# One-hots of a graph convolution compared as bf16 pairs, and three moved pieces of work beside a feed-forward

## The reference, cut to what matters

```python
h = segment_sum(h1[src] * norm, dst)          # first convolution, 8 features
h = relu(layernorm(h) ...)
out = relu(segment_sum((h @ W2)[src] * norm, dst) + b2)   # second convolution
x = x + out * size_factors
x = x + down(silu(gate(layernorm(x))) * up(layernorm(x)))  # 512 -> 1408 -> 512
```

## Time and profile before

| what | value |
|---|---|
| time, median of 3 runs | 3543.81 us (3538.64 to 3545.29) |
| time of the profiled execution | 3537.91 us |
| its span, first to last instruction | 3536.2 us |
| PE / DVE / ACT / POOL busy, share of the span | 79% / 56% / 30% / 58% |
| part with second convolution and feed-forward | about 802 to 2190 us |
| its one-hot comparisons (L171) | 49 times, 842.8 to 2040.3 us |

### The profile page before, as it was taken

How to read it: one execution, slowest core, us unless ns; L and a number is a source line. 1 busy time by engine, 2 the same in 40 slices (tenths; PEclk the granted TensorE clock), 3 DMA queues, 4 the chain that set the end, 5 groups by cost and what they waited for, 6 DMA issues and landing times. The chain is left out here.

```text
span 3536.2 us, 58101 instructions
## 1 busy us (share of the span) xinstructions
PE 2806.9 (79%) x16521; PEld 2050.4 (58%) x16522; DVE 1977.7 (56%) x3616; ACT 1074.2 (30%) x1721; POOL 2059.1 (58%) x2157
## 2 busy tenths in 40 slices
PE   6855655213999999999999996778887878788799
PEld 6855544212788877787878886333333434335687
DVE  8888898966354545454454543433344344443676
ACT  3445555003233323323233323001121212223454
POOL 0077777767777777777700001777777777772454
PEclk9678778556999999999999998899999999998899
DMA  3222232002233333333322324777777877775564
GB/s 104 59 63 53 49 100 46 5 4 53 46 105 96 100 90 105 91 85 101 85 90 92 102 83 135 219 225 232 224 235 238 244 231 244 233 242 174 174 212 129
DMA packets 237217, 459.14 MB, mean 130 GB/s; under 512 B 80060, under 2 KB 102828, under 8 KB 236994
## 3 DMA queue, kind: packets, MB, share of 16 engines
q0 software_dynamic: 111360, 235.84, 25.8%
q1 hardware_dynamic: 125634, 220.46, 19.2%
HBM read 389.41 MB, written 73.25 MB: 131 GB/s over the span
## 5 line engine op out<-in xcount | busy, mean ns | idle before, releaser
L1814 POOL DMA_INDIRECT rows<-xn_rows,srcT x784 | 742.3, 947 | 273.1 <-issue 244.8
L122 POOL DMA_INDIRECT msg_c<-hid_rows,srcT x752 | 727.4, 967 | 244.1 <-issue 230.1
L1965 PE MATMUL pV<-rows,oh 128*128 x2240 | 554.9, 395 | 144.7 <-issue 49.6
L122 POOL DMA_INDIRECT msg_b<-hid_rows,srcT x464 | 455.0, 981 | 149.3 <-issue 137.7
L1965 PEld LDWEIGHTS pV<-rows,oh 128*128 x2240 | 223.8, 100 | 461.6 <-issue 290.2
L1388 PE MATMUL acc<-wd,hT 128*128 128x512 f32 x1617 | 399.6, 395 | 0.0
L1363 PE MATMUL pG<-xT,wgu_hi 128*128 128x512 f32 (+1 forms) x1232 | 373.1, 385 | 10.1 <-issue 8.4
L1363 PE MATMUL pU<-xT,wgu_hi 128*128 128x512 f32 (+1 forms) x1232 | 362.9, 376 | 0.0
L1388 PEld LDWEIGHTS acc<-wd,hT 128*128 128x128 f32 x1617 | 301.3, 188 | 67.9 <-issue 8.8
L2278 DVE SCALAR_TENSOR_TENSOR oh<-ids,bases,dstT 128x896 f32 x160 | 184.2, 1151 | 211.0 <-issue 145.4
L2266 DVE TENSOR_TENSOR agg<-agg,pV x161 | 110.2, 685 | 335.7 <-PE pV L1965 335.3
(11 more groups left out here) (393 smaller groups left out, 4549.7 us busy)
## 6 DMA issues: line engine op xcount, KB each, us to landing
wd<-wd_rows SPq DMA_DIRECT2D x154, 512.0 KB, 3.6
we<-in_L_ffn_expert_w SPq DMA_DIRECT2D x16, 1024.0 KB, 8.4
x_rows<-xr SPq DMA_DIRECT2D x49, 256.0 KB, 4.6
xn_rows<-pair SPq DMA_DIRECT2D x49, 256.0 KB, 2.0
rows<-xn_rows,srcT POOLq DMA_INDIRECT x784, 3.8
res<-x_rows SPq DMA_DIRECT2D x49, 256.0 KB
x_rows<-agg SPq DMA_DIRECT2D x49, 256.0 KB, 4.3
xt<-in_x SPq DMA_DIRECT2D x48, 256.0 KB, 2.7
```

Source lines behind the costliest of these rows:

```text
L122: nc.gpsimd.indirect_dma_start(msg[:, c, :], None, table, bass.IndirectOffsetOnAxis(ap=srcT[:, c:c + 1], axis=0)).then_inc(landed[u % 2], 16)
L1814: nc.gpsimd.indirect_dma_start(rows[:, u % RING, c, :], None, xn2_rows, bass.IndirectOffsetOnAxis(ap=srcT[:, u * Q + c:u * Q + c + 1], axi ...
L1965: last = nc.tensor.matmul(pV[:, ds(to, 1), :].rearrange("p a d -> p (a d)"), oh[:, ds(to, 1), c, :].rearrange("p a d -> p (a d)"), rows[:, ...
```

## The change

Four things. (1) In the second convolution only, a unit first subtracts the tile's first row number (`first_id`, one fp32 per partition) from 20 numbers of `dstT` and writes them as bf16 (`rel`); the comparison then has two bf16 operands in SBUF, `numbers` (0 to 127, each twice) and `rel`, and is laid out so that two chunks lie side by side: the innermost dimension is the pair. After each tile 128 is added to `first_id` instead of to `tiota`. (2) The matmuls take a chunk's matrix from the pairs, at every second element. (3) `tile_range` of a unit moves out of `build` into `prepare`, which in the steps lies between DVE's product and its difference; these are now two functions, `up` and `low`. (4) `scale_rows` moves from (1, 1) to (2, 0), which is behind the build at (1, 2), and `rows` from (2,0), (3,0), (4,0), (5,0) to (3,0), (3,1), (4,0), (4,1).

```diff
@@ build_unit, with c0 and units as arguments
         nc.vector.tensor_tensor(lo, rest[:], mid, ALU.subtract)
-        nc.vector.tensor_tensor(onehot[:], bc(tiota.unsqueeze(1), (P, U, P)),
-                                bc(dstT[:, at].unsqueeze(2), (P, U, P)), ALU.is_equal).then_inc(ready, 1)
+        nc.vector.tensor_scalar(rel, dstT[:, at], first, None, ALU.subtract).then_inc(related, 1)
+        dve.wait_ge(related, n + 1)
+        full = (P, U // 2, P, 2)
+        nc.vector.tensor_tensor(onehot, bc(numbers.unsqueeze(1), full), bc(rel.rearrange("p (g j) -> p g j", j=2).unsqueeze(2), full),
+                                ALU.is_equal).then_inc(ready, 1)
@@ sum_columns
-            last = nc.tensor.matmul(acc[j * HX:j * HX + H3, :], mstage[:, k, :], onehot[:, k, :], start=False, stop=False)
+            last = nc.tensor.matmul(acc[j * HX:j * HX + H3, :], mstage[:, k, :], onehot[:, k // 2, :, k % 2], start=False, stop=False)
@@ groups
-    first = {(FB - 1, 2): [(part.build, 0)]}
+    first = {(FB - 1, 0.5): [(part.prepare, 0)], (FB - 1, 2): [(part.build, 0)]}
+        (j, 0.5): [(part.prepare, j)] for j in (1, 2, 3)} | {
-    behind = {(2 + j, 0): [(part.rows, j)] for j in range(4)} | {
+    behind = {(3 + j // 2, j % 2): [(part.rows, j)] for j in range(4)} | {
         (0, 0): [(part.residual, None)],
         (0, 2): [(part.stats_rows, None)],
-        (1, 1): [(part.scale_rows, None)]}
+        (2, 0): [(part.scale_rows, None)]}
             part.up(i, g, f)
+            beside(f, 0.5)
+            part.low(i, g, f)
             beside(f, 1)
@@ tensors and VectorE of the part
-            tiota = pb(ctx, "tiles_c", [P, 512], F32)[:, 0:P]
+            first_id = sb(ctx, "first_id", [P, 1], F32)
+            numbers = sb(ctx, "numbers_c", [P, P, 2], BF16)[:]
+            rel = sb(ctx, "rel_c", [P, U], BF16)[:]
+            pairs = onehot[:].rearrange("p u n -> p (u n)").rearrange("p (g n j) -> p g n j", n=P, j=2)
-                own.step(nc.vector.tensor_copy(tiota, iota[:]))
+                own.step(nc.vector.tensor_copy(numbers, bc(iota[:].unsqueeze(2), (P, P, 2))))
+                own.step(nc.vector.memset(first_id[:], 0.0))
+                def prepare(i, k, j):
+                    at_tile.append(tile_range(dve, ranges, i * G + k))
-                    own.step(nc.vector.tensor_scalar_add(tiota, tiota, float(P)))
+                    own.step(nc.vector.tensor_scalar_add(first_id[:], first_id[:], float(P)))
```

More of the change, by code:

```diff
@@ L152, in chunk_at, with build_unit @@
     return ds(at, size)
-def build_unit(nc, dve, t, units_done, ranges, dstT, tiota, onehot, msg, rest, mstage, split, ready, used, msg_ready):
-    c0, units = tile_range(dve, ranges, t)
+def build_unit(nc, dve, c0, units, units_done, dstT, first, numbers, rel, onehot, msg, rest, mstage, split, related, ready, used, msg_ready):
     with dve.Fori(0, units) as b:
@@ L310, with __init__ @@
 class Part:
-    def __init__(self, gate=nothing, up=nothing, down=nothing, build=nothing, sums=nothing, layer1=nothing,
+    def __init__(self, gate=nothing, up=nothing, low=nothing, down=nothing, prepare=nothing, build=nothing, sums=nothing, layer1=nothing,
                  stats=nothing, scale=nothing, norm=nothing, turn=nothing, residual=nothing, stats_rows=nothing, scale_rows=nothing,
@@ L316, in __init__ @@
                  enter=nothing, leave=nothing):
-        self.gate, self.up, self.down = gate, up, down
+        self.gate, self.up, self.low, self.down = gate, up, low, down
+        self.prepare = prepare
         self.build, self.sums, self.layer1 = build, sums, layer1
@@ L1171, in program @@
             "tail lanes ohs prod masked reduced parts far small_in nv_clear msg fence fence_sp fence_pe fence_dve onehot used split agg own_rows aggT conv relu "
-            "x1 var std rs xn xT_ps xT_hi xT_lo gate_ps up_ps silu hmul h_hi h_lo down x2 var2 std2 rs2 "
+            "related x1 var std rs xn xT_ps xT_hi xT_lo gate_ps up_ps silu hmul h_hi h_lo down x2 var2 std2 rs2 "
             "xn2 row_hi row_lo dve".split())}
@@ L1336, in sums @@
                         wait_alone(pe, s["aggT"], T, s["fence_pe"])
-                    sum_columns(nc, pe, T, units_done, ranges, own_rows[:, j, :], mstage, identb, zerob, acc, onehot,
+                    sum_columns(nc, pe, T, units_done, ranges, own_rows[:, j, :], mstage, identb, zerob, acc, pairs,
                                 s["onehot"], s["used"]).then_inc(s["agg"], 1)
@@ L1516, in _ @@
                 units_done = tally(dve, "units_done2")
+                at_tile = []
+                def prepare(i, k, j):
+                    at_tile.append(tile_range(dve, ranges, i * G + k))
                 def build(i, k, j):
@@ L1521, in build @@
                     nc.vector.tensor_copy(own_rows[:, j, :], own3[:, ds(T, 1), :].rearrange("p a b -> p (a b)")).then_inc(s["own_rows"], 1)
-                    build_unit(nc, dve, T, units_done, ranges, dstT, tiota, onehot, msg, mrest, mstage, s["split"], s["onehot"], s["used"], s["msg"])
-                    own.step(nc.vector.tensor_scalar_add(tiota, tiota, float(P)))
+                    build_unit(nc, dve, *at_tile.pop(), units_done, dstT, first_id[:], numbers, rel, pairs, msg, mrest, mstage, s["split"], s["related"], s["onehot"], s["used"], s["msg"])
+                    own.step(nc.vector.tensor_scalar_add(first_id[:], first_id[:], float(P)))
                 def layer1(i, k, j):
@@ L1573, in up, with low @@
                     nc.vector.tensor_tensor(sil[:, 0:n], pU[:, 0:n], sil[:, 0:n], ALU.mult).then_inc(s["hmul"], 1)
+                def low(i, g, f):
+                    step, n, slot = steps_before(i, g, f), len(GROUPS[g]) * P, (g * FB + f) % 2
                     dve.wait_ge(s["hmul"], step + 2)
@@ L1597, in rows @@
                     nc.vector.tensor_tensor(pair[:, k % 2, 1, :], xn[:, j % 2, :], pair[:, k % 2, 0, :], ALU.subtract).then_inc(s["row_lo"], 1)
-                groups(dve.Fori, Part(build=build, layer1=layer1, stats=stats, scale=scale, turn=turn, up=up,
+                groups(dve.Fori, Part(prepare=prepare, low=low, build=build, layer1=layer1, stats=stats, scale=scale, turn=turn, up=up,
                                       residual=residual, stats_rows=stats_rows, scale_rows=scale_rows, rows=rows,
```

## The result

The changed kernel takes 3506.22 us (median of 6 runs, 3500.2 to 3516.2), the kernel before 3539.37 us beside it (6 runs, 3530.4 to 3545.3). By the medians that is 33 us less. The ratio is 0.9911, 95% interval 0.9894 to 0.9929, which is 25 to 38 us of 3539: faster, and clear of the scatter. The profiled execution takes 3501.57 us, against 3537.91.

What follows compares the result with a forecast made beforehand. PE sets the time (busy 1108 of 1152 us), waiting for DVE's late one-hots. From 3537.9 us, 4.6 (first four tiles) and 32.7 (six groups) leave 3500.6; plus 5.9 for the median, 3506.5, said as 3507; range 3490 to 3524.

Steps and rivals of the forecast that it cites:

- Register work, 0.65: DVE's builds: moving tile_range's load and register operations into prepare takes 0.65 us off the gap before the first cast.
- A build, 5.60 to 3.85: DVE's build of a one-hot: 5.60 us less 0.65 register work, less 1.32 comparison, plus 0.22 rel, makes 3.85.
- The start of the chain, left at 1186.9: Step 2 of a three-tile group: build 1 starts at 1186.9, ready at 1190.75, before PE comes at 1192.16.
- The waits of 1.25 in step 4 and 1.3 before `layer1` 0: Three-tile groups: PE waits 1.25 us for one-hot 3, then 1.3 before layer1 0 for ACT's late copy.
- rival (b): Three-tile groups: no new waits in steps 4 and 5, 15 us less, 3492 in all; chance 0.15.
- First four tiles, 4.6: Serial tiles before the first group: shorter builds gain 4.8 us, less 0.2 for new constants, so 4.6.
- No port blocking: DVE's comparison beside POOL's gathers: two SBUF inputs cause no blocking, counted as nothing; by the skill's rule, near 3519.
- Rival (c): DVE's comparison stands behind a gather, up to 0.94 us each, 12 us in all, 3519; chance 0.08.
- (d): PE's one-hot matmuls: four strided streams read at half rate, 14 us, some of it hidden, 3519; chance 0.10.
- (g): PE's one-hot matmuls: four column groups lose their overlap, 20 take 1.17 us instead of 0.29, 3550; chance 0.02.
- Rival (e): SP's queue in three-tile groups: wd comes late by 1.5 us in six groups, 3516; chance 0.07.
- (f): DVE's comparison: the fast form isn't taken, a build is 5.2 us, perhaps 6 us remain, 3538; chance 0.03.

Runs made afterwards that it cites:

- experiment 4: Changed kernel with the register work (tile_range) back in build: steps 2 to 6 of six three-tile groups 235.0 us, ratio 0.9937 to the kernel before.
- experiment 3: Changed kernel with the old comparison (fp32 row numbers in PSUM, no pairs): steps 2 to 6 of six three-tile groups 239.9 us, ratio 0.9931 to the kernel before.
- experiments 5 to 7: Changed kernel with scale_rows back, 225.7 us; changed kernel with rows back, 226.0; kernel before with row numbers in SBUF, 257.3 and 257.1 (steps 2 to 6, six groups).

## Why the prediction was right, point by point

The time (3507 against 3506.2), the sign and the reason (DVE's one-hots came late, and a shorter build takes the waits away) were right. Its picture of steps 4 and 5 was not.

- **Comparison, 1.49 us; `rel`, 0.22.** 1.49 in the median and 0.23. The pair rate of L533 and L535 carried over exactly.
- **Register work, 0.65.** Mis-sized: put back, it costs 0.7 to 0.9 a build, as experiment 4 shows. The load and the operations of the earlier trace rows sum to 0.52, and the gaps beside them were put too low.
- **A build, 5.60 to 3.85.** In the group shown it is 3.6 (1185.61 to 1189.20) for build 1, 3.3 for build 2 (behind the difference that ends at 1193.56) and 3.1 for build 3 (behind the remainder that ends at 1201.56). The three are 0.3 to 0.7 short of 3.85 each, 1.6 together.
- **The start of the chain, left at 1186.9.** The prediction let build 1 start where the difference of step 1 had ended, 1.26 us behind the beginning of step 2. It has no term for build 0, which lies in the last step of the group before and gets shorter too. DVE comes to `residual` 2.2 us earlier against the gate of step 1 (1177.34 with the gate at 1179.33; 1174.86 with the gate at 1179.03), and the difference of step 1 ends at 1185.61, only 0.30 behind step 2. That is 0.96 us more for the chain, and the second to fifth of the six groups agree: 1.26 to 1.36 before, 0.27 to 0.30 after. From DVE's timelines, before and after:

```profile
1177.34 2.48 DVE L1582 TENSOR_TENSOR xr<-xr,acc 128x512 f32<-128x512 f32 x4
...
1174.86 2.48 DVE L1600 TENSOR_TENSOR xr<-xr,acc 128x512 f32<-128x512 f32 x4
```

- **The waits of 1.25 in step 4 and 1.3 before `layer1` 0.** This is the step that failed. One-hot 3 was expected 1.25 us after PE and came 0.9 before it (1204.69, PE at 1205.61). Counted from the beginning of step 2 it came after 19.4 us instead of 21.4. The start of the chain explains 1.0 of the 2.0 us and the shorter builds up to 1.6; about 0.5 was lost again where DVE waits for ACT. ACT began its copy for `aggT` at 1208.11, not at 1210.7, so that `layer1` began at 1208.51. Step 4 took 6.95 instead of 8.05 and step 5 8.81 instead of 9.7. Experiments 3 and 4 have both waits, so the mechanism is real; with 0.7 to 0.9 us more in each build they are back. The groups gained 39.8 where 32.7 were forecast. In this point rival (b), no new waits, was right, though it had priced them at 15 us, and step 5 still takes 8.81.
- **First four tiles, 4.6.** 3.35. The first two distances are 4.83 and 4.84, as worked out (4.8). The first tile gained 0.5 where 0.9 was counted, and the fourth came 5.42 behind the third, since its chunks were not there: its cast waited 1.19 us, by the profile for POOL's message count (L118).
- **No port blocking.** Wrong, and cheap; I had read the earlier trace rows by their median. In the changed kernel's timeline:

```profile
1186.73 0.94 POOL L122 DMA_INDIRECT msg_c<-hid_rows,srcT  x1 [0.30 <-issue]
1187.70 1.50 DVE L173 TENSOR_TENSOR onehot<-numbers_c,rel_c 128x2560 bf16<-128x2560 bf16 x1
1187.98 2.03 POOL L122 DMA_INDIRECT msg_c<-hid_rows,srcT  x1 [0.31 <-issue]
```

The gather that starts 0.28 into the comparison ends 0.81 behind it. Of 41 that started during one, 40 did so, and the comparison took 1.49 to 1.55 all the same. The kernel before already had this, beside the short L1576 of the earlier trace rows (1186.32, 0.56 us), where a gather took 1.33 us and ended 0.82 behind it:

```profile
1186.37 1.33 POOL L122 DMA_INDIRECT msg_c<-hid_rows,srcT  x1 [0.30 <-issue]
```

  So the "most" of 1441 in the earlier trace rows was the sign. The Trainium skill, SBUF — State Buffer, "Who interferes with whom", has the rule that a DVE instruction with two SBUF inputs contends with a GpSimd instruction that reads SBUF, and that the one that came first blocks the other; the trace agrees in the direction where the comparison is first. In the other direction no comparison took more than 1.545 us; short casts did take longer, as the last section shows. The price fell on the gathers, and the prediction's own sign of it is there: 127 of the 752 take more than 1 us, against 73 before. All 752 together went from 727 to 762 us, and the last began 1001 us into the part instead of 970. That they are needed later hides it, except perhaps for some of the 0.6 us at the fourth tile. Rival (c) had the blocking on the wrong engine, and at 12 us.
- **Matmuls at every second element, nothing.** Right: from the 20 matmuls to the next gate it is 0.50 us (1191.68 to 1192.18), against 0.60 before, and in the first four tiles, where they start from a wait in both kernels, the 20 take 0.72 us in both the earlier trace rows. Rivals (d) and (g) fall.
- **`wd` in time.** Right: PE has no wait for it. Rival (e) falls, and (f) with the 1.49.

How the number came out: by its own terms the profiled execution was to lose 37.3 us. The groups gave 7.1 more, the first tiles 1.25 less, the other steps and the end 1.5 more, and the part began 8.3 later. That sums to 36.3, so part of the closeness is luck: the groups were under-forecast by 7 us, and the late start of the part made up for it. The 5.9 us added for the median were 4.65 in the result (3506.22 against 3501.57). Over the runs the gain is 25 to 38 us, and the part's own gain by the profiles is 44; the difference lies in front of the part or is scatter there. Its start moves by up to 17 us between profiles, also between two of one kernel; why, is left open, and so is whether the change has a small share in it.

## What to carry to other kernels

When one engine sets the time and another feeds it late, cost the feeder's whole chain through several steps, and begin with the work before the first wait, which the change may have made shorter too: 0.3 to 0.7 us a build, three builds in a row, and a start 1 us earlier decided whether two waits existed at all. Moving work alone only chooses which step waits (4 us here). Making the late work shorter takes the waits away: the faster comparison gave 23 us by itself, and the register work 18 on top of the moves, so it counts like engine work. Read the longest of a line's durations as well as its median: it is where contention shows.

## What the runs showed of the hardware

- **A gather is held by a DVE instruction with two SBUF inputs for all that is left of it, and 0.81 to 0.83 us more**, where that is longer than its own 0.94. It holds for comparisons with 2-byte and 4-byte inputs and for short differences; of the 232 gathers that started during a comparison with one input in PSUM (77, 77 and 78 in both profiles of the kernel before and in experiment 3) none was held.
- **In the other direction, short casts are held by a gather.** In the kernel before, 15 of the 98 casts of the builds (L164, L168) took 0.28 to 0.49 us instead of 0.24. All 15 began 0.53 to 0.73 us behind the start of a gather, and ended 1.01 to 1.04 behind it; no cast without a gather beside it took more than 0.246. From the timelines of POOL and DVE:

```profile
1199.34 0.94 POOL L122 DMA_INDIRECT msg_c<-hid_rows,srcT  x1 [0.30 <-issue]
...
1199.90 0.45 DVE L164 CAST mstage<-msg_c 128x160 bf16 x1 [1.13 <-issue]
```

- **Faster and slower chips, one program.** On the two chips of experiments 5 to 7 the kernel before takes 5420 and 5435 us instead of 3540. PE's timeline in the changed kernel's first unit of the grouped steps shows single matmuls 2 to 3 us apart, with no releaser:

```profile
2251.20 0.22 PE L226 MATMUL pB<-onehot,mstage 128*24 128x128 bf16 x1 [2.27 <-issue]
2254.01 0.26 PE L226 MATMUL pB<-onehot,mstage 128*24 128x128 bf16 x1 [2.58 <-issue]
2256.11 0.27 PE L226 MATMUL pB<-onehot,mstage 128*24 128x128 bf16 x1 [1.84 <-issue]
```

  The first two steps of the grouped part take 58.6 and 115.6 us there, against 8.51 and 8.48 on the faster chip, and the third 10.84 against 8.99. Behind them the means of steps 2 to 6 agree with the faster chip within 0.1 us in the changed kernel, so its sums can be compared. Between the two profiles of the changed kernel 1873 us are to be placed: 554 lie in front of the part, 788 between its start and the first gate, 157 between the first and the last gate, nearly all in those first steps, and 375 behind the last gate, spread over the rest of the kernel. What the chip waits for there no run shows.
- **Gathers beside the groups cost the kernel before some 3 us; row numbers in SBUF give little.** With its row numbers in SBUF the old kernel takes 257.1 and 257.3 where the kernel before takes 262.2 and 262.3, but the first two ran on slower chips, where no gather runs beside the six groups. In the sixth group no gather runs in any of them: there steps 2 to 6 take 43.43 and 43.35 us in the kernel before and 43.11 and 43.10 with the row numbers in SBUF. Of these 0.3 us the addition to them (299 to 226 ns) gives 3 x 0.07 = 0.2. The second to fifth groups of the kernel before, with gathers beside them, take 44.1 to 44.3, 0.7 to 0.9 more than its sixth, while with the row numbers in SBUF and no gathers the second to sixth are all 43.1 to 43.2. So the gathers are the likely cause of most of the 5 us; with gathers and the row numbers in SBUF together no run was made. The kernel before was not profiled on a slower chip, which would show the edit by itself.
